# Down projection of the sparse FFN as three products of rounded halves, the weights split by ScalarE and GpSimd

## The reference

```python
x = x + xattn(layernorm(x), ctx, Wq, Wk, Wv, Wo)     # 32 heads, 2048 context rows and the 128 latents
x = x + mamba(layernorm(x), in_proj_w, ...)          # 8 groups of 16 heads, width 8192
x = x + ffn(layernorm(x), c1_w, c2_w, w1, w2t)

def ffn(x, c1_w, c2_w, w1, w2t):                     # INTER = 1792, blocks of 32
    inter = x @ c1_w.T @ c2_w.T
    idx = argmax(inter in blocks of 32) + block start
    h = relu(w1[idx] . x)                            # one unit of each block
    return h @ w2t[idx]
```

## Time and profile before

| | us |
|---|---|
| median of 3 runs | 628.72 (627.93 to 629.59) |
| span of the profiled execution, first to last instruction | 626.9 |
| TensorE busy (matmuls) | 614.3 (98%) |
| VectorE busy | 442.4 (71%) |
| ScalarE busy | 332.7 (53%) |
| GpSimd busy | 225.4 (36%) |

### The profile page before, as it was taken

The page is one execution under the profiler, slowest core; times in us unless marked ns, Lnnn a source line. Parts: engine busy times, 40 slices in busy tenths (PEclk is TensorE's granted clock), DMA queues, the critical chain, the costliest instruction groups (busy, mean ns, idle before and its releaser), DMA issues.

```text
span 626.9 us, 11014 instructions
## 1 busy us (share of the span) xinstructions
PE 614.3 (98%) x3916; PEld 525.9 (84%) x3916; DVE 442.4 (71%) x881; ACT 332.7 (53%) x613; POOL 225.4 (36%) x169
## 2 busy tenths in 40 slices
PE   8999999999999999999999989999999999999997
PEld 7888888899898989899988989997979779787573
DVE  4533138678888888888886669789794774958773
ACT  2413115668676867686766537664544554447110
POOL 0000002269778877887786612225012021100000
PEclk9999999999999999999999999999999999999999
DMA  8500011878887788778769929375765857787500
GB/s 258 228 1 26 8 37 44 216 189 215 213 213 201 202 211 214 201 201 215 178 168 246 354 104 309 138 300 194 261 254 202 295 209 259 249 362 301 203 1 17
DMA packets 29533, 120.61 MB, mean 192 GB/s; under 512 B 7680, under 2 KB 8064, under 8 KB 21936
## 3 DMA queue, kind: packets, MB, share of 16 engines
q1 hardware_dynamic: 28912, 118.96, 61.4%
q10 hardware_dynamic: 576, 1.05, 0.6%
HBM read 86.30 MB, written 0.26 MB: 138 GB/s over the span
## 4 chain that ended last, share of the span: by engine, by line
PE 81%; POOL 5%; DVE 5%; ACT 3%; issue 3%; DMA 1%; DVEq 0%; SPq 0%; ACTq 0%
PE ps L1745 20%; PE ps L1444 11%; PE ps L1445 10%; PE ps L1446 10%; PE ps L1785 9%; PE ps L1545 4%; POOL pt_lo L534 3%; PE ps L1621 2%; PE ps L1774 2%; PE ps L1895 2%; PE ps L1505 2%; POOL v_lo L534 2%; PE ps L1858 2%; DVE prob_far L1096 2%; DMA ring<-wk_dram 1%
## 5 line engine op out<-in xcount | busy, mean ns | idle before, releaser
L1745 PEld LDWEIGHTS ps<-norm_t,ring 128*128 128x128 f32 x1152 | 131.7, 192 | 4.9 <-issue 4.1
L1745 PE MATMUL ps<-norm_t,ring 128*128 128x128 f32 x1152 | 133.2, 276 | 0.0
L534 POOL TENSOR_TENSOR pt_lo<-far_t,pt_hi 128x512 fp32r<-128x512 f32 (+1 forms) x94 | 111.7, 1213 | 54.9 <-ACT pt_hi L638 54.9
L712 ACT ACTIVATE prob_far<-prob_far,neg_max 128x1024 f32<-128x1024 f32 (+2 forms) x96 | 85.5, 892 | 55.0 <-DVE neg_max L1100 55.0
L1096 DVE TENSOR_SCALAR_CACHE_REDUCE prob_far<-ps 128x256 f32<-128x256 f32 (+2 forms) x96 | 86.7, 906 | 32.0 <-PE ps L1446 31.6
L1275 DVE SCALAR_TENSOR_TENSOR acc<-raw,cw,acc 128x127 f32<-128x127 f32 (+2 forms) x240 | 83.4, 421 | 18.8 <-ACT acc L889 18.2
L1120 DVE STREAM_TRANSPOSE prob_far<-prob_far 128x2176 f32<-128x2176 f32 x30 | 73.1, 2437 | 0.8 <-ACT prob_far L712 0.2
L612 POOL TENSOR_SCALAR_AFFINE_SELECT at_hi<-a_hi 128x2048 fp32r<-128x2048 f32 x8 | 16.1, 2011 | 133.9 <-PE ps L1757 102.8
L1444 PE MATMUL ps<-pt_hi,v_hi 128*128 128x256 f32 x208 | 61.2, 294 | 2.7 <-POOL pt_lo L534 2.3
L1444 PE MATMUL ps<-k_hi,q_hi 128*128 128x512 f32 (+2 forms) x160 | 61.4, 384 | 1.4 <-ACT v_all L638 0.7
L1446 PE MATMUL ps<-pt_lo,v_hi 128*128 128x256 f32 x208 | 58.7, 282 | 0.0
(11 more groups left out here) (220 smaller groups left out, 1146.5 us busy)
## 6 DMA issues: line engine op xcount, KB each, us to landing
ring<-w_in_dram SPq DMA_DIRECT2D x36, 1024.0 KB, 4.9
far_t<-prob_far SPq DMA_DIRECT2D x240, 136.0 KB, 2.6
ring<-w_out_dram SPq DMA_DIRECT2D x16, 1024.0 KB, 4.9
ring<-wq_dram SPq DMA_DIRECT2D x16, 512.0 KB, 4.2
ring<-wo_dram SPq DMA_DIRECT2D x16, 512.0 KB, 3.7
w_sb<-w_dram SPq DMA_DIRECT2D x4, 896.0 KB, 9.2
ring<-ctx_t_dram SPq DMA_DIRECT2D x3, 1024.0 KB, 5.6
ring<-w_dram SPq DMA_DIRECT2D x3, 1024.0 KB, 9.0
```

The source lines that it names most:

```text
L534: sub = lambda dst, a, hi: pool.tensor_tensor(dst, a, hi, ALU.subtract)
L712: nc.scalar.activation(tile, tile, ACT.Exp, bias=neg_max[:, b, h:h + 1], accum_out=part_sum[:, b, h, i:i + 1]).then_inc(exp_ok, 1)
L1745: ins = mm(ps[:, bank, t * T:t * T + T], w[:, t, c, :], norm_t[:, c, :], start=(c == 0), stop=(c == NC - 1))
```

## The change

Twelve of the fourteen blocks of the down projection become three rounded products each. For these

- ScalarE copies each of the three slots of w2 to `w2_hi` (fp32r, 128 x 2048). The first copy stands before `squares(7)`, the other two between `squares(7)` and the root of L979.
- GpSimd subtracts: `ring_lo = ring - w2_hi`, 128 x 2048, in the ring's own place, three times; each waits for its copy alone.
- At each of the first three turn-overs ScalarE makes two copies, `hsel_hi` and `hsel_t`, and GpSimd the difference `hsel_lo` (128 x 512) from both.
- TensorE: `down_hi`, `down_w2_lo`, `down_h_lo` in place of one float32 product per slot. The last two blocks stay plain float32. `turn_over(3)` moves ahead of `down_h_lo(2)`.

`w2_hi` 0 and 1 lie where `at_hi1`, `at_lo1` were, `w2_hi` 2 where `decay1` was: hence the waits on `seg_ps` and `y_ps`.

```diff
+            for i in range(3):                                   # GpSimd, behind all it had
+                slot = stream(FFN0 + i)[0]
+                pool.wait_ge(w2h_ok, i + 1)
+                sub(ring_lo[slot][:], ring[slot][:], w2_hi[i][:].bitcast(F32)).then_inc(w2l_ok, 1)
+            for i in range(3):
+                pool.wait_ge(ht_ok, i + 1)
+                sub(hsel_lo[:, 4 * i:4 * i + 4, :], hsel_t[:, 4 * i:4 * i + 4, :],
+                    hsel_hi[:, 4 * i:4 * i + 4, :].bitcast(F32)).then_inc(hl_ok, 1)
...
+            def w2_split(i):                                     # ScalarE
+                slot, before = stream(FFN0 + i)
+                act.wait_ge(landed[slot], 16 * (before + 1))
+                copy(w2_hi[i][:], ring[slot][:]).then_inc(w2h_ok, 1)
+
+            act.wait_ge(seg_ps, 2 * GROUPS)
+            w2_split(0)
             squares(GROUPS - 1)
+            w2_split(1)
+            act.wait_ge(y_ps, GROUPS)
+            w2_split(2)
             act.wait_ge(var_s, 4)
...
                 act.wait_ge(ht_ps, i + 1)
+                if i < 3:
+                    copy(hsel_hi[:, 4 * i:4 * i + 4, :],
+                         ps[:, i, :].rearrange("p (c t) -> p c t", t=T)).then_inc(hh_ok, 1)
                 copy(hsel_t[:, 4 * i:4 * i + w, :],
...
-            for i in range(4):                                   # TensorE
-                if 0 < i < 3:
-                    turn_over(i + 1)
-                s, before = stream(FFN0 + i)
-                pe.wait_ge(landed[s], 16 * (before + 1))
-                pe.wait_ge(ht_ok, i + 1)
-                for t in range(4 * i, min(4 * i + 4, NFT)):
-                    ins = mm(ps[:, 4, :], hsel_t[:, t, :], ring[s][:, (t % 4) * DM:(t % 4 + 1) * DM],
-                             start=(t == 0), stop=(t == NFT - 1))
+            def down(i, turned, weights, first=False):
+                for t in range(4):
+                    mm(ps[:, 4, :], turned[:, 4 * i + t, :], weights[:, t * DM:(t + 1) * DM], start=first and t == 0,
+                       stop=False)
...
+            down_hi(0)
+            down_w2_lo(0)
+            down_h_lo(0)
+            turn_over(2)
+            down_hi(1)
+            down_w2_lo(1)
+            down_h_lo(1)
+            down_hi(2)
+            down_w2_lo(2)
+            turn_over(3)
+            down_h_lo(2)
+            s, before = stream(FFN0 + 3)
+            pe.wait_ge(landed[s], 16 * (before + 1))
+            pe.wait_ge(ht_ok, 4)
+            for t in range(12, NFT):
+                ins = mm(ps[:, 4, :], hsel_t[:, t, :], ring[s][:, (t % 4) * DM:(t % 4 + 1) * DM], start=False,
+                         stop=(t == NFT - 1))
```

More of the change, by code:

```diff
@@ L86 @@
 RING = 6
+SPLIT_FT = 12
 SLOT = 2048
@@ L249, in build @@
                     final = sbuf(st5, "final", [P, DM])
+                    sbuf(st5, "final_end", [P, 3296])
+                    hsel_hi = sbuf(st5, "hsel_hi", [P, SPLIT_FT, T], F32R)
+                    hsel_lo = sbuf(st5, "hsel_lo", [P, SPLIT_FT, T], F32R)
                 raw = [sbuf(st4, f"raw{b}", [P, 4, T]) for b in range(2)]
@@ L256, in build @@
                 sg.append(sbuf(st4, "sg1", [P, TPG, T]))
+                with ExitStack() as same_place:
+                    w2_late = sbuf(same_place, "w2_hi2", [P, SLOT], F32R)
                 decay.append(sbuf(st4, "decay1", [P, HPG, T]))
@@ L262, in build @@
                 ug = [sbuf(st4, f"ug{b}", [P, TPG, T]) for b in range(2)]
+                with ExitStack() as same_place:
+                    w2_hi = [sbuf(same_place, f"w2_hi{i}", [P, SLOT], F32R) for i in range(2)] + [w2_late]
                 at_hi.append(sbuf(st4, "at_hi1", [P, HPG, T], F32R))
@@ L312, in build @@
         ffn_ps, final_ok = sem("ffn_ps"), sem("final_ok")
+        w2h_ok, w2l_ok, hh_ok, hl_ok = sem("w2h_ok"), sem("w2l_ok"), sem("hh_ok"), sem("hl_ok")
         w1_in, w1h_ok, w1l_ok, nh_ok, nl_ok = (sem("w1_in"), sem("w1h_ok"), sem("w1l_ok"), sem("nh_ok"),
@@ L1887, in _, with down_hi, down_w2_lo, down_h_lo @@
             turn_over(1)
-            for i in range(4):
-                if 0 < i < 3:
-                    turn_over(i + 1)
-                s, before = stream(FFN0 + i)
-                pe.wait_ge(landed[s], 16 * (before + 1))
-                pe.wait_ge(ht_ok, i + 1)
-                for t in range(4 * i, min(4 * i + 4, NFT)):
-                    ins = mm(ps[:, 4, :], hsel_t[:, t, :], ring[s][:, (t % 4) * DM:(t % 4 + 1) * DM],
-                             start=(t == 0), stop=(t == NFT - 1))
+            def down(i, turned, weights, first=False):
+                for t in range(4):
+                    mm(ps[:, 4, :], turned[:, 4 * i + t, :], weights[:, t * DM:(t + 1) * DM], start=first and t == 0,
+                       stop=False)
+            def down_hi(i):
+                pe.wait_ge(hh_ok, i + 1)
+                pe.wait_ge(w2h_ok, i + 1)
+                down(i, hsel_hi, w2_hi[i], i == 0)
+            def down_w2_lo(i):
+                pe.wait_ge(w2l_ok, i + 1)
+                down(i, hsel_hi, ring_lo[stream(FFN0 + i)[0]])
+            def down_h_lo(i):
+                pe.wait_ge(hl_ok, i + 1)
+                down(i, hsel_lo, w2_hi[i])
+            down_hi(0)
[15 more added lines that the diff above has]
+                         stop=(t == NFT - 1))
             ins.then_inc(ffn_ps, 1)
```

## The result

The changed kernel takes 642.78 us (median of 4 runs, 642.1 to 643.73), the kernel before in the same comparison 628.86 us (4 runs). The ratio is 1.0229, 95% interval 1.0217 to 1.0242: slower by 13.9 us. Predicted were 642.3 us, range 637 to 645. The profiled execution has a span of 640.9 us and a time of 642.91; the span before was 626.9.

The account below looks back on a forecast made before the run. TensorE, busy for 98% of the span at full clock, was taken as the bound. The terms -1.96 + 12.5 + 2.1 + 1.0 = +13.6 us on 628.7 gave 642.3 us, range 637 to 645.

Parts of the forecast that it names:

- TensorE's saving: Down projection: twelve blocks at 0.70 us as three rounded products instead of 0.86, 1.96 us less.
- When the splits run: Before and beside `gate(7)`: first w2 copy done at 585.15, GpSimd subtracting three times 4.5 us, 585.2 to 598.7.
- the root half a microsecond late: ScalarE's root at 590.65: the third copy may push it by half a us, costed at nothing beside `out_proj(7, 1)`.
- The stop: At `gate(7)`: three gate instructions each wait for a GpSimd subtraction, so TensorE stands still 12.5 us before `out_proj(7, 0)`.
- (b): Rival at the gate: VectorE and GpSimd run side by side, no block, 626.8 us; chance 0.10.
- (c): Rival at the gate: GpSimd gives way, only `w1_split(3)` is caught, `res` 3 to 8 us late, 631 to 637; chance 0.08.
- The sum over one tensor: VectorE's sum over `ysq` behind the gate (1.90 us), assumed to run free beside GpSimd.
- The clock: Behind the stop, in `out_proj(7, 0)`: four us at half rate lose 2.1 us, bounds 0 and 3.5.
- The mask: Third turn-over: GpSimd's short subtractions delay VectorE's two-input mask instructions, TensorE waits 1.0 us for `hsel`, bounds 0 and 1.3.

Follow-up runs that it names:

- the paced run: The change with GpSimd's w2 subtractions placed between VectorE's excluded instructions, VectorE subtracting half of slot 2, and cast, root and turn-over moves: 626.37 us, ratio 0.9971.
- the run with memsets: The change with GpSimd's three w2 subtractions replaced by memsets of the same place, started at the same moment: 628.64 us, ratio 1.0005.
- the early cast: The change with GpSimd's subtractions after the whole gate, plus VectorE's cast of the mask's ranks moved ahead of `skip_add(7)`: 630.15 us, ratio 1.0031.
- the run with the root first: The early cast kernel with ScalarE's third w2 copy behind the root instead of ahead of it: 630.38 us, ratio 1.0038.

## Why the prediction was right, point by point

1. **TensorE's saving, -1.96.** Right: 0.23 us a product (4.62 us for 20), and 12.69 - 10.73 in the paced run.
2. **When the splits run.** Right within 0.4 us: GpSimd began at 584.83, the gate at 584.87, both somewhat earlier than I had them, and each subtraction took 4.5 us as the slope of the earlier trace rows gave. I had the first gate instruction slip through and the second to fourth caught; the first three were caught and the fourth ran free. It makes no difference to the sum: in both cases the three subtractions fall within the first four gate instructions. I had the root half a microsecond late and at no cost; it was 0.8 late where no stop hid it (`w1_split(3)` at 591.78 in the run with memsets), and cost nothing there.
3. **The stop, +12.5.** Right, 12.6. The mechanism was read from two instructions at 429 us and is shown by three runs: with the subtractions behind the gate it is gone, with memsets at the same moment it is gone, and with one subtraction one instruction is caught. Rivals (b), side by side, and (c), GpSimd giving way, fall with the profile itself. The runs add that neither engine always gives way: with GpSimd after the gate, it was GpSimd's second subtraction that waited for `w1_split(3)`, issued 0.27 us before it. The sum over one tensor was taken as free, and it is (1.98 us beside a subtraction).
4. **The clock, +2.1.** Right in kind, a little too small: 2.45 in the profile, 2.2 by the runs in which TensorE was kept busy. The size was read from the kernel's start; the stretch at half speed behind the stop was a little longer.
5. **The mask, +1.0.** The wait was 1.05, on the instructions named, at 1.50 and 1.10 us; its price was 1.25, since the turn-over behind it took 0.2 more.

The terms that were too small come to 0.7 us; 0.3 of that was made good by an earlier start of the gate in the profiled execution, which differs from one execution to the next (584.1 to 585.4 in the profiles). So the total looks a little better than its parts.

The expectations of two experiments were too low by 1 and 2 us, both for the same two reasons. I followed the excluded instruction that I had in mind and not every instruction of VectorE up to `res` and `norm_lo`: a cast of 32 columns and `w1_split(3)` were as exclusive as the gate. And I gave no price to a low clock behind the wait for `normed`: behind waits of only 1.9 and 2.9 us it cost 2.9 and 2.5 us, where the waits themselves had grown by 1.6 and 2.5. In what I expected of the early cast this led to a wrong mechanism, a pause of TensorE for the cast, which the trace does not have.

## What to carry to other kernels

"GpSimd is idle there" is not enough to give it a subtraction: before moving work to it, list every VectorE instruction in that stretch with two SBUF inputs, and every cast and `tensor_scalar` from SBUF to SBUF, and count each as able to wait for a whole GpSimd instruction. A row of the old trace in which a short VectorE instruction takes as long as the GpSimd one beside it shows that before anything is built. Then place the long work by semaphores between such instructions, in pieces shorter than the gaps, or let VectorE do it in its own idle time. And where TensorE gets a new wait, even of 2 us, look at the granted clock behind it before pricing it at its length.

## What the runs showed of the hardware that I had not expected

- GpSimd holds up a cast of 128 x 32 for 4.50 us (0.17 alone), and a memset, which reads nothing, holds up the same cast (1.85) and a `tensor_scalar` (1.11 for 0.55), but not `tensor_tensor` or `scalar_tensor_tensor` with two SBUF inputs.
- At the seam between two GpSimd instructions `w1_split(3)` got through when it had been issued 0.3 us and 1.0 us before the first one's end (two profiles), and did not when it was issued 0.02 us before. With work placed so, the same kernel has runs 5 us apart.
- When VectorE's instruction is first, GpSimd's waits: a subtraction of 4.5 us took 6.29 beside `w1_split(3)`.
- TensorE's clock fell to half in a run with no single stop of more than 2.0 us: with GpSimd after the gate TensorE had 3.05 us of work between 594 and 599 us and was at half speed from 599 to 605.7. With a stop of the same length and 2.85 us of work in the same stretch, the profile of the run with the root first shows full clock throughout, while the other four runs of that kernel have a mean granted clock of 0.995 to 0.997, so it seems to have fallen in them. What decides between them is open.
